# Second attention: scores made a second time with the keys in the partitions, in place of turning the probabilities

## The reference

```python
q = (query @ w_q.T).reshape(B, T_q, N_HEADS, HEAD_DIM)        # 16 heads of 32
k = (kv_source @ w_k.T).reshape(B, T_kv, N_HEADS, HEAD_DIM)   # 120 keys
v = (kv_source @ w_v.T).reshape(B, T_kv, N_HEADS, HEAD_DIM)
attn = jax.nn.softmax(jnp.einsum('bqhd,bkhd->bhqk', q, k) * HEAD_DIM ** -0.5, axis=-1)
out = jnp.einsum('bhqk,bkhd->bqhd', attn, v).reshape(B, T_q, D_MODEL)
return out @ w_o.T
```

## Time and profile before

| | us |
|---|---|
| median of 3 runs | 1251.64 |
| lowest and highest run | 1249.28, 1256.03 |
| span of the profiled execution | 1257.6 |
| PE busy in the span | 1189.3 |
| DVE busy | 950.4 |
| ACT busy | 708.7 |
| POOL busy | 589.7 |

### The profile page before, as it was taken

How to read it: one execution, slowest core, us unless ns; L and a number is a source line. 1 busy time by engine, 2 the same in 40 slices (tenths; PEclk the granted TensorE clock), 3 DMA queues, 4 the chain that set the end, 5 groups by cost and what they waited for, 6 DMA issues and landing times.

```text
span 1257.6 us, 29419 instructions
## 1 busy us (share of the span) xinstructions
PE 1189.3 (95%) x10692; PEld 822.8 (65%) x10692; DVE 950.4 (76%) x2006; ACT 708.7 (56%) x1988; POOL 589.7 (47%) x685
## 2 busy tenths in 40 slices
PE   6888998799999999999999999999999998799996
PEld 3555665588888888786444445777777776466663
DVE  5889898899999999896677777777777775445460
ACT  4377788799899999896344322222222231365552
POOL 0047668737666667733200000445544345466744
PEclk9999999999999999999999999999999999899999
DMA  9522033134445454643870141221314320799987
GB/s 346 210 60 76 1 32 46 43 111 142 165 135 169 159 172 148 181 157 119 153 196 1 41 127 34 68 44 60 69 34 108 96 68 2 220 254 242 256 139 96
DMA packets 157567, 150.28 MB, mean 119 GB/s; under 512 B 78544, under 2 KB 111472, under 8 KB 157424
## 3 DMA queue, kind: packets, MB, share of 16 engines
q1 hardware_dynamic: 139584, 125.94, 35.5%
q0 software_dynamic: 13248, 21.15, 8.9%
q10 hardware_dynamic: 4592, 1.32, 0.6%
HBM read 84.93 MB, written 57.19 MB: 113 GB/s over the span
## 4 chain that ended last, share of the span: by engine, by line
PE 59%; DMA 17%; issue 8%; DVE 8%; POOL 5%; ACT 3%; ACTq 0%; SPq 0%; POOLq 0%; DVEq 0%
PE bank L121 28%; DMA lists<-att_land 14%; PE bank L1503 6%; PE bank L2125 5%; PE bank L955 4%; POOL lists L1629 4%; PE bank L1435 4%; PE bank L1456 3%; PE bank L1450 2%; PE bank L1421 2%; DMA q_rows<-att_land 1%; PE bank L1024 1%; ACT att_land L1353 1%; PE bank L872 1%; PE bank L891 1%
## 5 line engine op out<-in xcount | busy, mean ns | idle before, releaser
L1629 POOL DMA_INDIRECT lists<-att_land x128 | 134.4, 1050 | 310.7 <-DVE att_land L1770 166.8
L1353 ACT ACTIVATE att_land<-bank,att_land 128x120 f32<-128x120 f32 x512 | 178.3, 375 | 11.3 <-DVE att_land L1221 11.2
L2125 PE MATMUL bank<-att_land 128*128 128x512 f16 x768 | 177.3, 381 | 0.6 <-DVE program_logits L1304 0.6
L1952 ACT ACTIVATE att_land<-program_x 128x512 f32<-128x512 f32 x40 | 25.2, 631 | 195.2 <-DVE program_x L2094 165.1
L2125 PEld LDWEIGHTS bank<-att_land 128*128 128x128 f16 x768 | 75.4, 98 | 82.9 <-issue 2.0
L121 PE MATMUL bank<-program_xs,program_wgu 128*128 128x512 f16 x576 | 128.7, 379 | 0.6 <-DVE att_land L1729 0.6
L1353 ACT ACTIVATION_READ_ACCUMULATOR att_land<-bank,att_land 128x1 f32 x512 | 112.8, 221 | 0.0
L121 PE MATMUL bank<-att_land 128*128 128x128 f16 (+1 forms) x1560 | 101.0, 221 | 0.5 <-DVE att_land L1278 0.5
L121 PEld LDWEIGHTS bank<-program_xs,program_wgu 128*128 128x128 f16 x576 | 56.2, 98 | 67.5 <-DVE att_land L1729 1.1
L1221 DVE TENSOR_REDUCE att_land<-bank 128x4 f32<-128x480 f32 x128 | 82.4, 644 | 20.5 <-PE bank L1421 20.1
L1503 PE MATMUL bank<-att_land 128*128 128x512 f16 x384 | 93.4, 379 | 0.0
(11 more groups left out here) (305 smaller groups left out, 2817.2 us busy)
## 6 DMA issues: line engine op xcount, KB each, us to landing
att_land<-q_rows SPq DMA_DIRECT2D x96, 128.0 KB, 2.6
xn_rows<-att_land SPq DMA_DIRECT2D x37, 256.0 KB, 3.7
out_rows<-att_land SPq DMA_DIRECT2D x37, 256.0 KB, 6.4
q_rows<-att_land SPq DMA_DIRECT2D x32, 256.0 KB, 2.9
xt_tiles<-att_land SPq DMA_DIRECT2D x32, 256.0 KB, 2.1
x_rows<-program_x SPq DMA_DIRECT2D x8, 1024.0 KB, 4.8
att_land<-x_rows SPq DMA_DIRECT2D x8, 1024.0 KB, 5.6
program_xs<-xt_tiles SPq DMA_DIRECT2D x28, 256.0 KB
```

What stands on the lines that cost most here:

```text
L1353: last = act.activation(prob[:, c, h, :], ps_s[c % 2][:, h, :], ACT.Exp, bias=nmax[:, u % 2, c, h:h + 1], accum_out=rsum[:, u % 2, n:n + 1])
L1629: pool.indirect_dma_start(out=io["lists"], out_offset=bass.IndirectOffsetOnAxis(ap=index[:, t, k:k + 1], axis=0), in_=load[:, t, k, :], in ...
L2125: last = pe.matmul(ps_y[i][:, :], hid[:, c % 2, a, i * P:(i + 1) * P], wd[:, q, c, :], start=c == 0 and n == 0, stop=c == NC - 1 and n == 2)
```

## The change

The probabilities are not turned any more. The scores are made twice. `scores` stays, only for the maxima, and `maximum` writes them negated. `maxima_transposed` turns the 16 maxima of a tile with one PE instruction, `maxima` on ACT copies them to float16, and SP writes them with one DMA as the 97th row of the packed queries; the 97th row of the keys is 1. `turned_scores` then makes the scores with the keys in the partitions, with the maximum already subtracted (four products of 97 rows for a group). `exps` is now two activations over 120x512: one writes the float16 high part, the second writes the exponential in place in PSUM. `prob_low` is as before. The value rows have a 33rd column of ones for each head, so that `outputs` also gives the row sums; because 16 x 33 columns don't fit a bank, head 0 has its own place in the bank of `ps_x`, with its own reciprocal (`inverse_sum0`) and its own scaling on ACT (`first_weighted`).

The packed queries have three slots in place of two. The orders in the `step` functions are new on all engines. `output_high` and `output_low` of a tile move from step u + 2 to the start of step u + 3, `gate_high` and `gate_low` from u + 4 to u + 5, the second half of `queries(u)` from the end of step u - 2 to the start of step u - 1. `turned_scores(u, 0)` and `(u, 1)` stand in step u + 1, `(u, 2)` and `(u, 3)` in u + 2. On SP, xt_tiles and the new DMA stand around q_rows, and xn_rows goes behind the packed queries. The number of steps is the same; PE's list in `TAIL` goes from 63, 65, 67, 67, 70, 71 to 65, 66, 67, 68, 70, 71.

The core of the diff; `packed_queries` also changes `u % 2` to `u % 3`, and `scores` waits for `max` of two groups earlier in place of `exp`:

```diff
+    nmax = g.early(SM, [P, 2, HC, KC])
-    nmax = g.early(SM, [P, 2, KC, HC])
-    prob = g.early(7 * D, [P, 4, HC, J])
...
+            r = t - 1
+            if live(r):
+                sp.wait_ge(s["n_ok"], r + 1)
+                need(sp, c4["t_mm"], KC * (r - 2))
+                to = g.queries[MAXROW, r % 3].rearrange("p r n -> p (r n)").rearrange("p (a n) -> p a n", n=P)
+                sp.dma_start(to, nmT[0:HEADS, r % 2, :]).then_inc(n_in[r % 2].handle, 16)
+            if live(u):
+                sp.wait_ge(q_out[u % 2], 16 * (u // 2 + 1))
+                need(sp, c4["t_mm"], KC * (u - 2))
+                need(sp, c4["s_mm"], KC * (u - 2) + 1 if u >= 2 else 0)
+                if u == 0:
+                    sp.wait_ge(f.a["sim"], NT)
+                packed_queries(sp, g, io, u, q_in)
...
-            if live(u):
-                sp.wait_ge(q_out[u % 2], 16 * (u // 2 + 1))
-                need(sp, c4["s_mm"], KC * (u - 1))
-                if u == 0:
-                    sp.wait_ge(f.a["sim"], NT)
-                packed_queries(sp, g, io, u, q_in)
...
         def step(t):
+            if t == 0:
+                pool.wait_ge(f.j_hi, f.jobs)
+                pool.wait_ge(f.j_lo, f.jobs)
+                pool.memset(g.vh[:, :, :, DH:DH + 1], 1.0).then_inc(fixed.handle, 1)
...
+        def inverse_sum0(u):
+            if live(u):
+                dve.wait_ge(c4["o_mm"], KC * u + 2)
+                need(dve, of0, u - 1)
+                dve.reciprocal(rinv[:, u % 2, 0:1], ps_o0[:, DH:DH + 1]).then_inc(inv0.handle, 1)
         def inverse_sums(u):
             if live(u):
-                dve.wait_ge(c4["exp"], KC * u + KC)
+                dve.wait_ge(c4["o_mm"], KC * u + KC)
                 need(dve, s["of"], u - 1)
-                dve.reciprocal(rinv[:, u % 2, :], rsum[:, u % 2, :]).then_inc(s["inv"], 1)
+                dve.reciprocal(rinv[:, u % 2, 1:HEADS].rearrange("p (h o) -> p h o", o=1), ps_o[:, :, DH:DH + 1]).then_inc(inv.handle, 1)
...
+            if live(u):
+                need(dve, inv, u + 1)
                 need(dve, s["o_tr"], u)
                 if u == 0:
                     dve.wait_ge(f.q["x_new"], NT)
-                dve.tensor_tensor(of[:, :].rearrange("p (h o) -> p h o", h=HEADS),
-                                  ps_o[:, :].rearrange("p (h o) -> p h o", h=HEADS),
-                                  rinv[:, u % 2, :].rearrange("p (h o) -> p h o", o=1).to_broadcast([P, HEADS, DH]),
+                dve.tensor_tensor(of[:, DH:D].rearrange("p (h o) -> p h o", h=HEADS - 1), ps_o[:, :, 0:DH],
+                                  rinv[:, u % 2, 1:HEADS].rearrange("p (h o) -> p h o", o=1).to_broadcast([P, HEADS - 1, DH]),
                                   ALU.mult).then_inc(s["of"], 1)
...
         def step(t):
-            maximum(t - 1, 3)
-            prob_low(t - 1, 0)
+            prob_low(t - 2, 1)
+            output_low(t - 3)
+            gate_low(t - 5)
             query_low(t + 1)
             rows_low(t + 2)
             yield
-            prob_low(t - 1, 1)
             maximum(t, 0)
-            weighted(t - 2)
             logits(t - 5)
+            prob_low(t - 2, 2)
             maximum(t, 1)
-            prob_low(t - 1, 2)
-            residual(t - 3)
-            gate_stats(t - 3)
-            maximum(t, 2)
             aggregate(ln, t + 5)
             stats(ln, t + 6)
             first_rows(t + 3)
-            prob_low(t - 1, 3)
-            output_low(t - 2)
+            prob_low(t - 2, 3)
+            inverse_sum0(t - 2)
+            maximum(t, 2)
+            inverse_sums(t - 2)
+            weighted(t - 2)
+            prob_low(t - 1, 0)
+            residual(t - 3)
+            maximum(t, 3)
+            gate_stats(t - 3)
             aggregate(lg, t - 3)
-            gate_low(t - 4)
-            inverse_sums(t - 1)
+            if t in (0, 1):
+                dve.wait_ge(f.j_hi, f.jobs)
+                if t == 1:
+                    dve.wait_ge(f.a["exp"], NT)
+                dve.memset(g.keys[MAXROW, t], 1.0).then_inc(row_ok.handle, 1)
             if t == 2:
                 dve.wait_ge(gw_hi, 1)
...
     def scalar(act):
-        def prob_high(u, c):
+        def exps(u, c):
             if not live(u):
                 return
-            act.wait_ge(c4["p_mm"], KC * u + c + 1)
+            act.wait_ge(c4["t_mm"], KC * u + c + 1)
             need(act, c4["o_mm"], KC * (u - 1) + PLACE[c] + 1)
             if u == 0 and c == 0:
                 act.wait_ge(f.a["x_new"], NT)
-            act.activation(pT[0:J, c, 0], ps_p[c % 2][0:J], ACT.Copy).then_inc(c4["p_hi"], 1)
-        def exps(u, c):
-            if not live(u):
-                return
-            act.wait_ge(c4["max"], KC * u + c + 1)
-            need(act, s["inv"], u - 1)
-            need(act, c4["p_mm"], KC * (u - 1) + c + 1)
-            for h in range(HC):
-                n = c * HC + h
-                last = act.activation(prob[:, c, h, :], ps_s[c % 2][:, h, :], ACT.Exp, bias=nmax[:, u % 2, c, h:h + 1],
-                                      accum_out=rsum[:, u % 2, n:n + 1])
-            last.then_inc(c4["exp"], 1)
+            act.activation(pT[0:J, c, 0], ps_p[c % 2][0:J], ACT.Exp)
+            act.activation(ps_p[c % 2][0:J], ps_p[c % 2][0:J], ACT.Exp).then_inc(c4["exp"], 1)
+        def maxima(u):
+            if live(u):
+                act.wait_ge(s["n_mm"], u + 1)
+                need(act, n_in[u % 2], 16 * (u // 2))
+                act.activation(nmT[0:HEADS, u % 2, :], ps_n, ACT.Copy).then_inc(s["n_ok"], 1)
+        def first_weighted(u):
+            if live(u):
+                need(act, inv0, u + 1)
+                need(act, s["o_tr"], u)
+                if u == 0:
+                    act.wait_ge(f.q["x_new"], NT)
+                act.activation(of[:, 0:DH], ps_o0[:, 0:DH], ACT.Copy, scale=rinv[:, u % 2, 0:1]).then_inc(of0.handle, 1)
...
         def step(t):
-            prob_high(t - 1, 0)
+            exps(t - 2, 1)
+            output_high(t - 3)
+            gate_high(t - 5)
             query_high(t + 1)
             rows_high(t + 2)
             yield
-            prob_high(t - 1, 1)
-            exps(t - 1, 3)
-            prob_high(t - 1, 2)
-            exps(t, 0)
-            exps(t, 1)
-            prob_high(t - 1, 3)
-            output_high(t - 2)
-            gate_high(t - 4)
-            exps(t, 2)
+            exps(t - 2, 2)
+            maxima(t - 1)
+            exps(t - 2, 3)
+            first_weighted(t - 2)
+            exps(t - 1, 0)
...
-        def prob_transposed(u, c):
+        def maxima_transposed(u):
+            if live(u):
+                pe.wait_ge(c4["max"], KC * u + KC)
+                need(pe, s["q_lo"], min(u + 3, NT))
+                pe.transpose(ps_n, nmax[:, u % 2].rearrange("p h c -> p (h c)"), g.ident[:, :]).then_inc(s["n_mm"], 1)
+        def turned_scores(u, c):
             if not live(u):
                 return
+            b = u // TB
+            if c == 0:
+                need(pe, n_in[u % 2], 16 * (u // 2 + 1))
             if u == 0 and c == 0:
+                need(pe, row_ok, 1)
                 pe.wait_ge(f.a["p_lo"], NT)
+            if u == TB and c == 0:
+                need(pe, row_ok, 2)
             if u == 0 and c == 1:
                 pe.wait_ge(f.a["y_ok"], NT)
-            pe.wait_ge(c4["exp"], KC * u + c + 1)
             need(pe, c4["p_lo"], KC * u + c - 1)
             for h in range(HC):
-                last = pe.transpose(ps_p[c % 2][0:J, h, :], prob[:, c, h, :], g.ident[:, :])
-            last.then_inc(c4["p_mm"], 1)
...
+                    need(pe, fixed, 1)
+            if c == 0:
+                need(pe, s["xt_lo"], min(u + 5, NT))
+                need(pe, s["o_lo"], u)
+                need(pe, s["l_ok"], u - 2)
             for h in range(HC):
-                cols = slice((c * HC + h) * DH, (c * HC + h + 1) * DH)
-                for n, (a, b) in enumerate(((0, 0), (0, 1), (1, 0))):
-                    last = pe.matmul(ps_o[:, cols], pT[0:J, c, a, h, :], g.v1[0:J, b, u // TB, cols],
-                                     start=n == 0, stop=n == 2)
+                n = c * HC + h
+                to = ps_o0 if n == 0 else ps_o[:, n - 1, :]
+                for k, (a, b) in enumerate(((0, 0), (0, 1), (1, 0))):
+                    if b:
+                        last = pe.matmul(to[:, 0:DH], pT[0:J, c, a, h, :], g.vl[0:J, u // TB, n * DH:(n + 1) * DH],
+                                         start=False, stop=False)
+                    else:
+                        last = pe.matmul(to, pT[0:J, c, a, h, :], g.vh[0:J, u // TB, n, :], start=k == 0, stop=k == 2)
             last.then_inc(c4["o_mm"], 1)
...
+                need(pe, s["n_ok"], u - 2)
...
                 pe.wait_ge(s["of"], u + 1)
-                need(pe, s["o_lo"], u)
-                need(pe, s["xt_lo"], min(u + 5, NT))
-                need(pe, s["l_ok"], u - 2)
+                need(pe, of0, u + 1)
...
```

(25 more changed lines are left out.)

111 lines of the change are left out of this document (64 added, 47 removed).

## The result

The changed kernel took 1285.6 us (median of 4 runs, 1280.6 to 1290.9) against 1253.7 us (4 runs, one more than above, 1249.3 to 1256.0): a ratio of 1.0267, 95% interval 1.0222 to 1.0312. The forecast was 1260 us, 1240 to 1275 us for 8 times in 10. The direction was right, the size wrong: +8 us forecast, +32 us measured.

The account below looks back on a forecast made before the run. PE's own work was taken to fill the step before, and a loop of waits through output_low after. Steps +8, start -3 and end +3 us made +8 on 1251.6: 1260 us, range 1240 to 1275 for 8 in 10.

Parts of the forecast that it names:

- the loop: Second attention: waits from turned_scores(0) through exps, prob_low, output_low, rows_transposed and back make a step 11.12 us.
- start -3: Before the second attention's steps: ACT's head exponentials leave, two memsets enter on DVE; -3 us, within -7 and +2.
- steps +8: Second attention: some 26 steps at 11.15 us in place of 10.84, +8 us.
- end +3: From tile 31's scores to the last logits: 39.9 us becomes 43, +3, within 0 and +7.
- the release of ACT: At the start, the last steps of `front` no longer wait on ACT for head exponentials, 2.69 us in one piece.
- The engines' sums: Work per attention step: PE 9.9 us, ACT about 6.4, DVE 10.2; by sums alone about 10.25 from 10.84.
- The in-place exponential: Second activation of exps, in PSUM: ends 0.60 us behind the first's end, bounds nothing and a full second.
- Its stalls: Attention steps: the old 0.13 us a step is not added again, and nothing is counted for the new DMA.
- The maxima's transfer: New DMA ahead of turned_scores(0): beyond 2.8 us it stalls PE; at 3.3, +13 us, 1273; chance 0.17.
- The gaps can take all 15.6 us: At the end, PE's gaps after the change hide all six placed parts of the shared expert, 15.6 us.
- My own walk, +10: End without the shared expert's parts, lists followed with their waits: 31 us long before, 41 after.
- the sums decide: Unseen slack lets the attention step fall to DVE's 10.25 us: 1236 us, up to 1245; chance 0.23.

Follow-up runs that it names:

- r4_reordered_more: r1_reordered with the fills of the keys' row on GpSimd and the token transfers issued by SyncE: 1246.0 us, ratio 0.995 to the kernel before.
- e6_no_wait: Changed kernel with turned_scores contracting 96 rows, no maximum subtracted, and waiting for the maxima's transfer three tiles late: 1285.5 us, ratio 1.0268.
- e5_memset_pool: Changed kernel with the two fills of the keys' row done by GpSimd instead of VectorE: 1284.2 us, ratio 1.0257.
- r1_reordered: Changed kernel with only the calls within a step of attention1 reordered on TensorE, VectorE and ScalarE: 1252.0 us, ratio 1.0001 to the kernel before.
- r6_reordered: Changed kernel with a second new order of the calls within a step of attention1, same instructions: 1276.8 us, ratio 1.0211.
- e4_tokens_sync: Changed kernel with the four token transfers issued by SyncE at the end of its step instead of by ScalarE: 1288.1 us, ratio 1.031.

## Why the prediction was wrong

Direction and the loop held, and all three terms of the sum were too low, each beyond the bounds it was given. By the three parts of the table, forecast and measured: start -3 (within -7 and +2) and +6.0, steps +8 (2.6 either way) and +16.7, end +3 (within 0 and +7) and +10.6. Together +8 and +33.3. Over the end's own window, from tile 31's scores to the last logits, it is 39.9 us forecast to become 43, and 52.0 measured. So the path was right and the terms were mis-sized, in three places: the step, whose loop was 0.14 us too short (3.5 us) and whose stalls were put at nothing (5.4 us); the start, where the release of ACT was booked as time gained; and the end, where the gaps were taken as cover for all 15.6 us of placed parts.

- *The engines' sums.* ACT left the race, as worked out. PE's sum, 9.9 us a step, was 0.2 too small: with TensorE the bound r4_reordered_more has base steps of 10.12 us. By the starts of its timeline the 16 turned scores take 0.94 us for 0.88, and the 12 other transposes 1.55 for 1.41. DVE's 10.2 held two waits of 0.13 that this order avoids, since it separates both pairs; without them it is 10.0, and DVE was busy 9.9. That a step of sums alone was possible, and about 10.25 long, was right; the order put on record with the change did not reach it.
- *The loop, 11.12 us.* Confirmed place by place. PE 0.45 for 0.42, ACT 1.12 for 1.13, DVE with the signal 3.98 for 3.88, PE again 5.74 for 5.69. The in-place exponential, for which there was no row, starts 0.49 behind the first and takes 0.59: the value taken. The 0.10 on DVE is that rows_transposed starts 0.14 after output_low's end (462.98 + 0.68), where I took 0.04. PE idles 0.63 before rows_transposed and 0.36 before gate_transposed, for 0.7 and 0.5. 25 times 0.14 (11.29 less 11.15) is 3.5 us.
- *Its stalls.* I compared a loop without stalls with a mean of before that had 0.13 us a step of them, and said that they would not come again. They were replaced: 3.45 us in the step of the token transfers, 2 us by the maxima's transfer, 5.4 in all. The first was missed altogether. I had put ScalarE's queue out of the race by its busy share, but its activations are links of the loop, and of the 4.72 us that its queue issues between two of them 3.45 show in the step. 8 + 3.5 + 5.4 is the 16.7 measured, to 0.2.
- *The maxima's transfer.* It landed in 1.6 to 3.7 us, median 2.4, for the 2.8 that the walk gave it: slack enough nearly always. e6_no_wait shows it: rival refuted, the low end of my bounds (0 us) being nearly right with 2 us in all.
- *The start, -3.* The step failed where it read the release of ACT (26.1 of 30 us busy) as time gained. ACT's busy time from 230 to 260 us did fall, to 14.9, but the time was not gained. Two things entered the chain of waits there, VectorE's first fill, 1.66 us and near the upper bound, and the first transfer of the maxima:

```profile
244.75 1.66 DVE att_land L1360
253.05 3.29 DMA att_land<-att_land
```

  And PE's clock fell: 0.89 in the mean from 230 us to the first issue, where it was 1.00 before. 0.11 of 64.3 us is 7 us of full clock, so by this estimate the clock alone could make up the 6. How they divide is open. Taking the fills away gave 1.5 us in e5_memset_pool, within the spread of equal starts; in e6_no_wait, where PE doesn't wait for the first three transfers, the first issue came no earlier (295.4). That the order has a part in it is shown by r1_reordered and the two kernels made from it, whose first issues come at 286.2 to 289.6 us, against 292.7 to 298.0 for the kernels with the changed kernel's order or one edit of it; r1_reordered has the fills still on VectorE. The second new order, r6_reordered, has 296.0.
- *The end, +3.* "The gaps can take all 15.6 us" is the step that failed. The shared expert's first products may run only behind n_ok of the last tile, and the longest gaps, 2.13 and 2.34 us ahead of product, lie before that. PE's timeline, the gaps and then the first two pieces:

```profile
592.88 2.19 PE L1558 MATMUL bank<-att_land 128*128 128x512 f16 x6 [2.13 <-DVE att_land L1325]
...
605.19 1.46 PE L1558 MATMUL bank<-att_land 128*128 128x512 f16 x6 [2.34 <-DVE att_land L1325]
...
612.85 2.75 PE L121 MATMUL bank<-program_xs,program_wgu 128*128 128x512 f16 x12
615.44 0.39 PE L1481 MATMUL bank<-att_land 97*120 97x128 f16 x4
615.67 2.75 PE L121 MATMUL bank<-program_xs,program_wgu 128*128 128x512 f16 x12
```

  The walk had 31 us before and 41 after, without the parts. With 15.6 us of parts these became 39.9 and 52.0: the gaps covered some 5 us after the change where 13.6 were forecast. The lower clock behind 592.88 is a small share of this, about 1 us by the starts of its rows. My own walk, +10, was thus near the measured +12.1; I overruled it by a cover that I had not placed gap by gap. Which of the two paths of nearly equal length would have to be shortened first was not tried.

Of the rivals, "the sums decide" priced a step of 10.25 us, and r1_reordered reached 10.12; it needed the order, not a hidden slack, and its end still kept it from the 1236 to 1245 us. The Trainium skill, "DMA: Bandwidth & Descriptors", "Why small descriptors are slow (HBM only)", exempts transfers within SBUF from the penalty of small pieces. The maxima's transfer, in pieces of 256 bytes, landed in 2.4 us, the 256 KB of q_rows in 2.1; that doesn't contradict the exemption, but no run moves the maxima in larger pieces. The Trainium skill, "ScalarE: Activation LUTs", in the part on what each stage is for, calls PSUM the destination with the lower latency. This trace shows 0.59 us in place in PSUM (float32) and 0.60 into SBUF (float16), no gain worth counting.

## What to carry to other kernels

When an edit takes work from an engine and also moves its calls, walk the new lists for loops before adding up durations: here 33.6 us, four times the forecast loss, lay between two orders of the same instructions. The loop that the walk found was good to 0.1 us a link; what such a walk leaves out (transfers on a queue, DMA issues between two links, other engines' slack) decides between orders that it rates alike, so run two. Work that is to be hidden in gaps must be placed gap by gap, with the wait that lets it start. And a difference of one or two us in a stretch where PE idles is read with the granted clock beside it.

## What the runs showed of the hardware

- A fill of one partition with 1920 float16 values takes VectorE 1.66 us, as long as three instructions on 128 partitions with 512 values each (0.57 to 0.60 each): that it is one partition saved nothing.
- Three token transfers issued by ScalarE took its queue 4.72 us, in which no activation began until 544.99; all four issued by SyncE took 3.79 us in e4_tokens_sync. A single xt_tiles issue takes SyncE 0.34 us: these four cost more than twice that each, on either queue.
- PE's clock at the start is not told by its busy time of the same stretch: from 245 to 260 us it was 1.00 before with PE busy 12.01 of 15 us, 0.77 in the changed kernel with 10.05, and 0.89 in r1_reordered with 9.21 and in r4_reordered_more with 10.86.
- Six products of 512 columns show 1.46 us at the full clock of 2.4 GHz, and 2.77 in a step of e6_no_wait whose granted clock is 0.70 in the mean: nearly the double, as at the lower level of 1.2 GHz.
